# Group norm and gate moved out of a recurrent scan and done per quarter of the batches in the feed forward stage

## The reference, cut to what matters

```python
g = jax.nn.silu(xg @ Wg.T)
...
_, out = jax.lax.scan(step, s0, rkvw)
og = out.reshape(b, l, h, s_)
m = og.mean(-1, keepdims=True)
va = ((og - m) ** 2).mean(-1, keepdims=True)
og = ((og - m) / jnp.sqrt(va + 1e-05)).reshape(b, l, e) * gn_w + gn_b
x1 = x + og * g @ Wo.T
xc = _ln(x1, ln2_w, ln2_b)
```

## Time and profile before

| | us |
|---|---|
| median of 3 runs | 1023.35 (1020.78 to 1023.88) |
| profiled execution, its own time | 1016.36 |
| its span, first to last instruction | 1014.6 |
| PE busy | 896.1 |
| DVE busy | 691.5 |
| POOL busy | 536.5 |
| ACT busy | 396.5 |

### The profile page before, as it was taken

One profiled execution on the slowest core, in us unless ns is written; L12 is line 12 of the kernel. 1 busy time (PEld: TensorE's weight loads), 2 busy tenths in 40 slices (PEclk: granted clock), 3 DMA queues, 4 the chain that ended last, 5 costly groups with the idle time before them and its releaser, 6 DMA issues.

```text
span 1014.6 us, 10745 instructions
## 1 busy us (share of the span) xinstructions
PE 896.1 (88%) x3588; PEld 398.5 (39%) x3588; DVE 691.5 (68%) x907; ACT 396.5 (39%) x819; POOL 536.5 (53%) x573
## 2 busy tenths in 40 slices
PE   1679978799786899688998999899998999979998
PEld 1233433343322343243343444344443454444454
DVE  6234499789988687888887698988998224442342
ACT  2013412333212241133223254565355554465395
POOL 2000388669987749648886778889682101000010
PEclk9687997899977899698999999999999999999999
DMA  7351679969689877878979844779642022001001
GB/s 270 134 125 73 179 178 222 233 171 233 162 187 216 209 184 196 212 145 224 243 182 281 216 112 100 183 192 227 163 99 83 21 73 83 21 4 39 21 0 42
DMA packets 100089, 150.69 MB, mean 149 GB/s; under 512 B 22850, under 2 KB 64066, under 8 KB 91842
## 3 DMA queue, kind: packets, MB, share of 16 engines
q1 hardware_dynamic: 73410, 129.03, 50.4%
q10 hardware_dynamic: 26624, 20.98, 8.5%
HBM read 115.38 MB, written 33.55 MB: 147 GB/s over the span
## 4 chain that ended last, share of the span: by engine, by line
PE 59%; DVE 14%; POOL 12%; issue 6%; ACT 5%; ACTq 2%; DMA 2%; SPq 0%; POOLq 0%; DVEq 0%
PE PS L1318 38%; PE PS L1381 4%; PE PS L1543 4%; POOL VB L704 4%; PE PS L1440 3%; PE PS L1520 2%; DVE PS L1033 2%; PE PS L1325 2%; POOL VB L699 2%; DVE VB L1150 2%; DVE M L1030 2%; DVE VB L1030 2%; POOL VB L695 2%; DVE M L1033 2%; PE PS L1454 1%
## 5 line engine op out<-in xcount | busy, mean ns | idle before, releaser
L1318 PE MATMUL PS<-M,W 128*128 128x512 f32 x672 | 329.8, 634 | 23.7 <-DVE M L1033 12.3
L1318 PEld LDWEIGHTS PS<-M,W 128*128 128x128 f32 x672 | 128.7, 202 | 198.2 <-issue 167.5
L704 POOL TENSOR_TENSOR VB<-VB 128x1024 f32<-128x1024 f32 x64 | 151.4, 2366 | 58.9 <-ACT VB L849 56.2
L1150 DVE TENSOR_TENSOR_SCAN VB<-PS,VB 128x512 f32<-128x512 f32 x128 | 149.1, 1206 | 25.9 <-POOL VB L704 17.3
L587 POOL TENSOR_SCALAR NM<-MV 128x2 f32<-128x2 f32 (+1 forms) x24 | 6.2, 258 | 283.7 <-DVE MV L1278 183.0
L1030 DVE TENSOR_TENSOR VB<-VB,PS 128x2048 f32<-128x2048 f32 x64 | 145.9, 2280 | 1.5
L695 POOL TENSOR_TENSOR VB<-KR,VB 128x1008 f32<-128x1008 f32 x64 | 129.7, 2026 | 17.5 <-DMA VB<-scr_vs 17.5
L699 POOL TENSOR_TENSOR VB<-WG,VB 128x1008 f32<-128x1008 f32 x64 | 129.3, 2020 | 0.0
L1033 DVE SCALAR_TENSOR_TENSOR PS<-PS,VEC,SX 128x512 f32<-128x512 f32 x80 | 60.2, 752 | 87.7 <-PE PS L1381 72.4
L1318 PE MATMUL PS<-W,M 128*128 128x512 f32 x224 | 105.1, 595 | 0.0
L1296 DVE TENSOR_REDUCE SM<-PS 128x1 f32<-128x512 f32 x64 | 44.0, 688 | 58.9 <-PE PS L1543 58.4
(11 more groups left out here) (167 smaller groups left out, 1280.5 us busy)
## 6 DMA issues: line engine op xcount, KB each, us to landing
VB<-scr_vs SPq DMA_DIRECT2D x64, 1024.0 KB, 7.9
W<-in_w SPq DMA_DIRECT2D x8, 1024.0 KB, 9.8
X<-in_x SPq DMA_DIRECT2D x4, 1024.0 KB, 8.2
scr_vs<-STG ACTq DMA_DIRECT2D x64, 64.0 KB, 5.7
scr_v<-STG ACTq DMA_DIRECT2D x16, 256.0 KB, 6.9
scr_w<-STG ACTq DMA_DIRECT2D x16, 256.0 KB, 8.3
scr_k<-STG ACTq DMA_DIRECT2D x16, 256.0 KB, 2.7
KR<-scr_k SPq DMA_DIRECT2D x16, 256.0 KB, 8.1
```

The costliest lines, as they stand in the source:

```text
L704: po.tensor_tensor(flat(bv[:, 0]), flat(bv[:, 0]), flat(bv[:, 1]), ALU.add).then_inc(g_kv, 1)
L1150: sc = dv.tensor_tensor_scan(s_, PS[:, 5, :], b_, 0.0, ALU.mult, ALU.add)
L1318: mm = pe.matmul(o, l, r, start=i == 0, stop=i == 3)
```

## The change

The group norm and the gate's arithmetic leave stream `end` and stream `p`. DVE's four operations finish OT, which is stored as it is. ACT only copies half of the gate's projection to STG. In stream `c`, for each quarter: ACT squares OG into SQ(q) (LS for q = 0, M2 for the others), PE averages with 16 matmuls of 128 columns, ACT adds EPS, POOL does the 13 operations on 128 columns and one masking product of 512 columns, PE spreads it with one matmul of 512 columns. Then DVE scales OG, ACT takes the tanh of the loaded gate into SQ, and DVE makes the gate and the product with the bias. All five order strings are written anew (in all, 24 fewer PE steps and 168 fewer POOL steps). A use of a staging slot after a `v` tile also waits for that tile's copies to scr_vs.

```diff
+    "l:7 c:1 l:1 l1:1 l:1 c:1 l:5 c:1 l1:1 l:2 c:2 l:2 c:2 l:8 c:3 l:4 c:1 l1:13 c:1 l1:14 l:2 l1:1 l:5 "
+    "c:1 l:1 c:3 l:2 c:12 l1:7 l:2 l1:1 l:2 l1:1 l:1 c:10 l:2 c:2 l1:1 c:3 l:1 c:1 l:6 l1:1 l:2 l1:3 l:4 "
...
+TAKES_C = [("var",), ("rstd",)] + [("wo", b) for b in range(4)] + [("tr", ec) for ec in range(4)] + [("fk", f) for f in range(4)]
...
+        def SQ(q):
+            return LS[:, 1] if q == 0 else M2[:]
...  POOL
-            def stream_end():
-                for bb in range(B):
-                    w.wait_ge(a_end, C4 + 2 * bb + 2)
-                    yield from newton(GR[:], GV[:], GT[:], g_end, 14 * bb)
+            def stream_n():
+                for q in range(NQ):
+                    w.wait_ge(a_gv, q + 1)
+                    yield from newton(GR[:], GV[:], GT[:], g_gn, 14 * q)
...
+                    po.tensor_tensor(btv(SQ(q)[:, 0, :]), GR[:].unsqueeze(1).to_broadcast([P, 4, L]),
+                                     MASK[:].unsqueeze(2).to_broadcast([P, 4, L]), ALU.mult).then_inc(g_gn, 1)
...  ACT
                 if f == 4:
-                    ac.activation(STG[:, ss, :], PS[:, n, :], ACT.Tanh, scale=0.5).then_inc(a_gt, 1)
+                    ac.activation(STG[:, ss, :], PS[:, n, :], ACT.Copy, scale=0.5).then_inc(a_gt, 1)
...
+            def norm_gate(q):
+                for m in range(4):
+                    w.wait_ge(d_og, 16 * (q + 1))
+                    w.wait_ge(p_fr, 4 * q)
+                    ac.activation(SQ(q)[:, m, :], OG(q)[:, m, :], ACT.Square).then_inc(a_sq, 1)
+                    yield
...
+                ac.activation(GV[:], PS[:, n, 0:L], ACT.Identity, bias=EB[:]).then_inc(a_gv, 1)
+                yield
+                for m in range(4):
+                    w.wait_ge(p_gn, 2 * q + 2)
+                    w.wait_ge(d_gl, 16 * (q + 1))
+                    ac.activation(SQ(q)[:, m, :], XN[:, m, :], ACT.Tanh).then_inc(a_gate, 1)
+                    yield
...  DVE
-            def gate(q, m):
-                stt(STG[:, ss, :], STG[:, ss, :], 1.0, PS[:, n, :], ALU.add, ALU.mult).then_inc(v_gst, 1)
...
-                    w.wait_ge(p_end, 3 * bb + 3)
-                    tt(OT[:], OT[:], PS[:, 7, 3 * L:4 * L].unsqueeze(1).to_broadcast([P, C4, L]), ALU.mult).then_inc(v_ot, 1)
...
+                for m in range(4):
+                    w.wait_ge(p_gn, 2 * q + 2)
+                    stt(O[:, m, :], O[:, m, :], vec(V_GNW + m), PS[:, n, :], ALU.mult, ALU.mult).then_inc(v_scl, 1)
+                    yield
+                for m in range(4):
+                    w.wait_ge(a_gate, 4 * q + m + 1)
+                    stt(G[:, m, :], G[:, m, :], 1.0, XN[:, m, :], ALU.add, ALU.mult).then_inc(v_gate, 1)
+                    yield
+                    w.wait_ge(v_gate, 4 * q + m + 1)
+                    w.wait_ge(v_scl, 4 * q + m + 1)
+                    stt(O[:, m, :], O[:, m, :], vec(V_GNB + m), G[:, m, :], ALU.add, ALU.mult).then_inc(v_y, 1)
+                    yield
...  PE, in stream_c ahead of wo
+                    w.wait_ge(a_sq, 4 * (q + 1))
+                    if q == NQ - 1:
+                        w.wait_ge(v_ot, 4 * B)
+                    for c in range(C4):
+                        for b in range(QB):
+                            mm = pe.matmul(PS[H * b:H * b + H, n, 0:L], SAME[:, 0], SQ(q)[:, c, b * L:(b + 1) * L],
+                                           start=c == 0, stop=c == C4 - 1)
+                    mm.then_inc(p_gn, 1)
+                    yield
+                    w.wait_ge(g_gn, 14 * (q + 1))
+                    n = banks.take(w, BANK_C[q, "rstd"], v_scl, 4 * (q + 1))
+                    pe.matmul(PS[:, n, :], SAME[:].rearrange("p g h -> p (g h)"), SQ(q)[:, 0, :], start=True,
+                              stop=True).then_inc(p_gn, 1)
+                    yield
```

More of the change, by code:

```diff
@@ L177 @@
 BANK_A.update({t: 2 + i % 2 for i, t in enumerate(TAKES_P)})
-TAKES_C = [("wo", b) for b in range(4)] + [("tr", ec) for ec in range(4)] + [("fk", f) for f in range(4)]
+TAKES_C = [("var",), ("rstd",)] + [("wo", b) for b in range(4)] + [("tr", ec) for ec in range(4)] + [("fk", f) for f in range(4)]
 TAKES_C += [(n, b) for b in range(4) for n in ("fr", "fv")]
@@ L326, in rwkv_attention_kernel @@
         p_tra, p_low, p_mix, p_td1, p_prj = [sem("p_" + n) for n in ("tra", "low", "mix", "td1", "prj")]
-        p_scan, p_wol, p_end = [sem("p_" + n) for n in ("scan", "wol", "end")]
+        p_scan, p_wol, p_end, p_gn = [sem("p_" + n) for n in ("scan", "wol", "end", "gn")]
         p_wo, p_trc, p_fk, p_fr, p_fv = [sem("p_" + n) for n in ("wo", "trc", "fk", "fr", "fv")]
-        v_sta, v_aga, v_sub, v_m1, v_mix, v_mad, v_gst = [
-            sem("v_" + n) for n in ("sta", "aga", "sub", "m1", "mix", "mad", "gst")]
+        v_sta, v_aga, v_sub, v_m1, v_mix, v_mad = [
+            sem("v_" + n) for n in ("sta", "aga", "sub", "m1", "mix", "mad")]
         v_sc, v_pr, v_kr2, v_ot, v_wm, v_hd = [
             sem("v_" + n) for n in ("sc", "pr", "kr2", "ot", "wm", "hd")]
+        v_gate, v_scl = sem("v_gate"), sem("v_scl")
         v_y, v_xa, v_stc, v_agc, v_subc, v_kr, v_rk, v_x2 = [
@@ L340, in rwkv_attention_kernel @@
             sem("a_" + n) for n in ("s0", "wr", "rg", "end", "wol")]
-        a_aff, a_xnc, a_exc, a_rl, a_kk, a_rr = [sem("a_" + n) for n in ("aff", "xnc", "exc", "rl", "kk", "rr")]
-        g_kv, g_wp, g_id, g_sel, g_sta, g_col, g_end, g_stc, g_colc = [
-            sem("g_" + n) for n in ("kv", "wp", "id", "sel", "sta", "col", "end", "stc", "colc")]
+        a_sq, a_gv, a_gate, a_xnc, a_exc, a_rl, a_kk, a_rr = [
+            sem("a_" + n) for n in ("sq", "gv", "gate", "xnc", "exc", "rl", "kk", "rr")]
+        g_kv, g_wp, g_id, g_sel, g_sta, g_col, g_gn, g_stc, g_colc = [
+            sem("g_" + n) for n in ("kv", "wp", "id", "sel", "sta", "col", "gn", "stc", "colc")]
         pf, pb, vf, vb, af, ab = [[sem(f"{n}{i}") for i in range(4)] for n in ("pf", "pb", "vf", "vb", "af", "ab")]
@@ L732, in stream_l @@
                     yield from mean_rstd(3 + ln, 2, gl_[ln], 4 * k, vf[ln], 4 * (k + 1))
-            weave(ORDER_POOL, {"a": stream_a(), "scan": stream_scan(), "end": stream_end(), "c": stream_c(),
+            weave(ORDER_POOL, {"a": stream_a(), "scan": stream_scan(), "n": stream_n(), "c": stream_c(),
                                **{n: stream_l(i) for i, n in enumerate(LANES)}})
@@ L868, in stream_end @@
                 yield
-                for bb in range(B):
-                    w.wait_ge(v_ot, 5 * bb + 4)
-                    w.wait_ge(p_end, 3 * bb + 1)
-                    w.wait_ge(a_rg, bb + 1)
-                    ac.activation(flat(KR[:, bb % 2, 1]), flat(OT[:]), ACT.Square).then_inc(a_end, 1)
-                    yield
-                    w.wait_ge(p_end, 3 * bb + 2)
-                    w.wait_ge(g_end, 14 * bb)
-                    w.wait_ge(g_id, 4)
-                    ac.activation(GV[:], PS[:, 7, 2 * L:2 * L + H], ACT.Identity, bias=EB[:]).then_inc(a_end, 1)
-                    yield
-            def affine(q, m):
-                w.wait_ge(d_og, 16 * (q + 1))
-                w.wait_ge(d_vec, 32)
-                ac.activation(OG(q)[:, m, :], OG(q)[:, m, :], ACT.Identity, scale=vec(V_GNW + m),
-                              bias=vec(V_GNB + m)).then_inc(a_aff, 1)
+            def norm_gate(q):
[3 more added lines that the diff above has]
+                    ac.activation(SQ(q)[:, m, :], OG(q)[:, m, :], ACT.Square).then_inc(a_sq, 1)
+                    yield
+                n = BANK_C[q, "var"]
+                w.wait_ge(p_gn, 2 * q + 1)
+                w.wait_ge(g_gn, 14 * q)
+                w.wait_ge(v_wm, 5)
+                w.wait_ge(g_id, 4)
+                ac.activation(GV[:], PS[:, n, 0:L], ACT.Identity, bias=EB[:]).then_inc(a_gv, 1)
[4 more added lines that the diff above has]
+                    ac.activation(SQ(q)[:, m, :], XN[:, m, :], ACT.Tanh).then_inc(a_gate, 1)
+                    yield
             def stream_c():
-                for m in range(C4):
-                    affine(0, m)
-                    yield
                 for q in range(NQ):
+                    yield from norm_gate(q)
                     w.wait_ge(g_stc, 4 * (q + 1))
@@ L920, in stream_c @@
                         yield
-                        if q + 1 < NQ:
-                            affine(q + 1, b)
-                            yield
             def stream_l(ln):
@@ L1134, in stream_a @@
                         yield from first_mix(q + 1)
-            def stream_p():
-                for q in range(NQ):
-                    for m in range(4):
-                        gate(q, m)
-                        yield
             def stream_scan():
@@ L1157, in stream_scan @@
                         w.wait_ge(d_kg[s], 16 * (bb // 2 + 1))
-                        w.wait_ge(p_end, 3 * bb - 2 if bb else 0)
+                        w.wait_ge(p_end, bb)
                         tt(RQ[:, :, 0:L], R, KR[:, s, 0], ALU.mult).then_inc(v_kr2, 1)
```

(26 more changed lines are left out.)

57 lines of the change are left out of this document (23 added, 34 removed), and 167 rows, old and new, of tables (ORDER_ACT, ORDER_DVE, ORDER_PE, ORDER_POOL).

## The result

The changed kernel takes **1057.9 us** in the median of its runs (1054.98 to 1064.37), the kernel before 1023.6 on the same chip: a ratio of 1.0349 (95% interval 1.0298 to 1.0401), 34 us slower. The forecast of 995 us and its range are both missed. The profiled execution took 1064.37 us.

A forecast was written before the change was run, and what follows sets the result against it. PE was taken as the bound, busy 896 of 1014.6 us. Terms -7 - 10 - 5 + 0 - 12 + 12 - 5 = -27 on 1016.4 gave 989; with 7 for the runs' median 996, given as 995, range 966 to 1022.

The forecast's parts named there:

- the last paragraph of the DVE part: DVE in the scan: twelve new two-SBUF-operand gates stretch by 4 us, taking back what left; 0 us, ends -5 and +25.
- the third rival: DVE and POOL: POOL's relief is hidden and contention on twelve gates eats the rest; median 1021 us, chance 0.15.
- The gains in the scan (-10, -5, -12, -5): Scan: PE's waits -10, DVE's idling for the gate's projection -5, POOL's relief -12, PE's clock -5 us.
- the -10 for PE's waits: PE's per-batch waits for ACT's squares, POOL's mask and DVE's 1/sqrt product vanish: -10 us, ends 0 and -10.
- the -12 for POOL: POOL in the scan loses about 41 us busy and most queue stops; a tenth of its 122 us: -12, ends 0 and -40.
- The gate's projection: DVE stood idle 18.3 us for it, scans and mixes queued behind; a quarter regained: -5 us, 0 to -18.
- The clock: PE from 120 to 480 us, granted 0.89: fewer gaps give some clock back, -5 us, 0 to -33.
- The new chain (+12): Norm and gate steps before each quarter's wo: 5 us in the tail, 2 to 3 per earlier quarter; +12, ends 0 and +78.
- PE work (-7): PE's variance and spreading matmuls: 15.3 us removed, 8 added; -7 us, ends -7 and +5.
- The check by the order: PE's work behind the last scan step: 182 us, plus 19 and 2; the 989 us puts that step at 786, 8 later.
- The first rival: The scan isn't held up at all, its last step staying at 777.6 us; median 971 us, chance 0.22.
- The second: Rival: the new chain before wo is the bound, 15 of its 19.5 us open per quarter; median 1044 us, chance 0.13.

The follow-up runs named there:

- 9: Kernel before without the group norm (gate kept), DVE's two-SBUF-operand instructions made one-operand copies in the first three quarters: 1000.5 us, ratio 0.9824.
- 8: Changed kernel with DVE's two-SBUF-operand instructions replaced by equally wide one-operand copies in the first three quarters: 1022.1 us, ratio 1.0022 to the kernel before.
- 7: Kernel before with DVE's two-SBUF-operand instructions replaced by equally wide one-operand copies in the first three quarters: 1011.6 us, ratio 0.9916.
- experiment 4: Kernel before, its orders and gate kept, with the group norm's squares, variance, POOL chain, spreading and 1/sqrt product left out: 1034.6 us, ratio 1.0134.
- 12: Neither norm nor gate, orders of the kernel before, DVE's two-SBUF-operand instructions made one-operand copies in three quarters: 1020.4 us, ratio 0.9983 to the kernel before.
- 10: Neither norm nor gate, orders of the changed kernel, DVE's two-SBUF-operand instructions made one-operand copies in three quarters: 1021.4 us, ratio 1.0014 to the kernel before.
- experiment 1: Changed kernel with its rewritten engine orders replaced by those of the kernel before, new steps put in where their inputs are there: 1097.0 us, ratio 1.0732.

## Why the prediction was wrong

**The sum, in the terms that the runs give.** The step from 9 to 8 is 1022.1 - 1000.5 = +21.6 us (the gate out of the scan, the products in a block, and the chain); the norm's leaving, from 7 to 9, -11.1; the meetings of DVE and POOL +23.8. Together +34.3, the measured difference, which is so by the way they are taken. Against them the forecast had -39 for everything that leaves the scan, +12 for the chain and 0 for the meetings.

**The step that failed most is the last paragraph of the DVE part**, "0 us (ends -5 and +25)". It looked for stretched durations in the twelve new gates of the scan, and of these it was right: the gates have means of 1222 ns (first quarter, LS<-LS,XN) and 825 (the others, M<-M,XN), which is 3.8 us above 0.69 each, where 4 were forecast. The stretching that costs the time struck instructions that the change doesn't touch: mixes and shift, +22.5 us of DVE time, on PE's way to its next matmuls. The runs put the meetings at +24 us, where the sum had nothing. The size 24 us lies within the end given; the place doesn't, and the third rival, which put the price on the gates, was right in name and size but not in place. The Trainium skill's rule (GPSIMD Engine Reference, "Specifications") that instructions with two SBUF inputs contend is borne out, far beyond what M<-M,XN showed: 9.92 us for four mixes in the timeline above. X<-STG,X at a maximum of 2814 ns was the true sign. The profile before also had M<-SX,VEC,EXT, at a mean of 868 ns with a least of 740 and a greatest of 2533, and the forecast left it out.

**The gains in the scan (-10, -5, -12, -5).** Without meetings they are real but smaller: the norm's leaving altogether gives 11.1 us, with 7 either way, and the instructions that it takes from PE have 15.3. So there is room for 3 us at most of the -10 for PE's waits and the -12 for POOL. POOL's term failed in its base: its 12% of the chain that ended last was read as time that its relief gives back. The chain after has 4% of POOL and is longer. With the meetings in place the norm's leaving is a loss of 12.5 us, as experiment 4 shows with nothing added. The gate's projection was no gain, because the row was misread: the group STG<-STG,PS holds the 16 gates and 16 products of the feed forward part, and the seven waits that make up the 18.3 us all stand before the latter, the first at 577.86 us, behind the last gate at 561.81. No DVE wait was open for the gate's projection. The clock went the other way, 0.85 where 0.89 had been. The Trainium skill's rule of a clock released by activity (TensorE: Matmul & The Clock Gate, "What's actually happening") agrees in its sign with these two executions, for PE's idle time in that stage was 59.7 us where it had been 56.6; but experiment 4 has 63.5 us of idle there at 0.89, so the sum of idle time alone doesn't give the clock.

**The new chain (+12).** Its parts were right but for the spreading: variance 1.08 us, POOL's steps 0.43 to 0.48 and 0.30, mask 1.04, 8.5 us on PE's clock between variance and spreading in the tail (908.30 + 1.08 to 917.86), waits on the mask 2.9 us in all, none of them in the tail, where 3.7 were expected. What was missed stands in the step from 9 to 12, 20 us: the affine and gate steps, "in the shadow of fr and fv" before, come out of it, and the gate leaves the scan. How the 20 us divide isn't shown; 13 of them at most are waits in front of wo, and only in the orders of before. Against the 21.6 us from 9 to 8 the term was short by 10. One unit in it isn't in the row that it names: a matmul is 0.90 us by the earlier trace rows (3.60 for four), not 0.86, which moves the cover in the tail by under half a microsecond.

**PE work (-7).** The new groups took 3.2 + 1.1 and 4.1 + 2.0 = 10.4 us, where 8 was said, so the term is -5 by its own rows. But PE's busy time rose by 12.6: all other instructions together took 17.5 us more, in a profile whose granted clock is lower.

**The check by the order** was half right: the tail behind the last scan step is 196.4 us where 203 was said. The scan's end was 866 instead of 786. Experiments 10 and 12 put 39 us on the move of work alone, for the same time, where the forecast had 8 and called it "fair for a scan that is itself relieved". The first rival (971) rested on the same belief. The second (chain as the bound, 1044) had the right side and a time 14 us from the result, but not the mechanism: no quarter has 10 us open on the mask or in front of wo. Its mechanism did come true in the orders of before (experiment 1), where PE waited 15.0, 17.2 and 6.7 us in front of wo.

**What stays open.** Why DVE and POOL meet more often once the norm is gone wasn't shown. It may be that POOL's 14 small steps and its standing idle for GV, 37 us before, were stretches in which DVE's two-operand instructions ran free; this is argued and not tested. No run changed only the phase of the two engines. Why 10, which has neither norm nor the gate's arithmetic, nor the replaced instructions, is some 20 us slower than 9 is open too. Nor was a version tried that keeps the kernel before and takes one operand of the mixes out of SBUF; experiment 7 puts what that could win at 9 us or less (0.84% of the time), for it replaces more than the mixes.

## What to carry to other kernels

Before crediting relief on one engine, look for the groups whose means stand above their minimum while it works: taking small steps from one engine can make its long instructions meet another engine's more often, and the loss then falls on groups that the diff doesn't touch. See also which instructions a row holds before pricing its waits: one name can cover two uses. A quantity gathered over a larger block is cheaper to compute and dearer to wait for: what was prepared slice by slice in the shadow of other work can then stand in one piece ahead of its reader. And a share of the chain that ended last is no price for what is removed from it; test it by leaving the work out, which here would have told the sign in one run.

## What the runs showed of the hardware that was not expected

Beside POOL's products of 1,008 and 1,024 columns, a mix with two SBUF operands that takes 0.75 us alone takes a median of 2.42 us and up to 2.82, about one for each product of POOL, and POOL's 2.0 us for 1,008 columns become 2.44. The update of X, 0.69 us alone, takes up to 2.87. With one SBUF operand, DVE's copies have a mean of 677 ns in the same kernels, and those products are back at 1996 to 2014 ns. POOL's small steps grow from 0.31 to 0.48 us between 32 and 128 columns, and the product with the mask takes 1.04 us for 512.
